# A chain of four attention layers on one core: high and low parts of small heads in every third row, and the maxima's rows sent by GpSimd

## The reference

```
L1: x = x + cross_attention(layernorm(x), ctx), 16 heads of 16; x = x + mlp(layernorm(x))
L2: x = attention(queries x, keys and values of concat(ctx, x)), 16 heads of 16, 512 keys, + residual; rmsnorm; mlp
L3: grouped attention, 32 query heads of 8 channels on 8 key heads, with an added mask; + residual; layernorm
attention: softmax(q k^T * scale + mask) v, all in float32
```

## Time and profile before

| | us |
|---|---|
| median of 3 runs | 1466.15 (1464.59 to 1468.97) |
| the profiled execution | 1463.16 |
| its span | 1461.9 |
| PE busy | 1295.2 (89%) |
| DVE busy | 902.7 (62%) |
| ACT busy | 722.1 (49%) |
| POOL busy | 456.4 (31%) |
| mean granted clock of TensorE | 0.916 |

### The profile page before, as it was taken

One profiled execution on the slowest core, in us unless ns is written; L12 is line 12 of the kernel. 1 busy time (PEld: TensorE's weight loads), 2 busy tenths in 40 slices (PEclk: granted clock), 3 DMA queues, 4 the chain that ended last, 5 costly groups with the idle time before them and its releaser, 6 DMA issues. The chain is left out here.

```text
span 1461.9 us, 26853 instructions
## 1 busy us (share of the span) xinstructions
PE 1295.2 (89%) x9901; PEld 1100.8 (75%) x9901; DVE 902.7 (62%) x2341; ACT 722.1 (49%) x1817; POOL 456.4 (31%) x843
## 2 busy tenths in 40 slices
PE   6999999999999999998777779776878898879795
PEld 6999999999999999987745458544545686556463
DVE  6966666698756666886755656545545455446461
ACT  5766656678656666672133442234534422434342
POOL 3544445454534544443321131210100211002101
PEclk9999999999999999999967799779877896989998
DMA  5310000033000000031333113155130222121200
GB/s 167 106 55 2 1 1 5 1 101 110 23 2 1 2 1 2 32 114 32 47 48 46 24 45 52 19 71 67 25 47 2 76 33 42 30 34 35 31 2 16
DMA packets 40356, 56.65 MB, mean 39 GB/s; under 512 B 5536, under 2 KB 20832, under 8 KB 40224
## 3 DMA queue, kind: packets, MB, share of 16 engines
q1 hardware_dynamic: 40224, 54.92, 18.6%
HBM read 32.68 MB, written 1.05 MB: 23 GB/s over the span
## 5 line engine op out<-in xcount | busy, mean ns | idle before, releaser
L1807 ACT ACTIVATE PT<-bank 128x512 f32<-128x512 f32 x320 | 174.6, 595 | 193.9 <-PE bank L1749 107.5
L1078 POOL TENSOR_SCALAR E<-E,rl 128x256 f32<-128x256 f32 x256 | 237.9, 941 | 0.0
L1871 DVE CUSTOM_DVE_ANT_0 Em<-bank,M 128x256 bf16<-128x256 f32 x256 | 95.1, 420 | 101.2 <-issue 65.8
L821 ACT ACTIVATE QTh<-bank,bqs 128x256 fp32r<-128x256 f32 x128 | 60.7, 474 | 182.1 <-PE bank L117 182.1
L1864 DVE TENSOR_REDUCE nm<-bank 128x1 f32<-128x512 f32 x128 | 82.3, 684 | 94.1 <-PE bank L1718 93.9
L1076 POOL TENSOR_TENSOR pb<-E,rl 128x2 f32<-128x2 f32 x128 | 33.7, 263 | 326.6 <-DVE rl L954 326.6
L1903 POOL CAST np<-nm 128x8 fp32r<-128x8 f32 (+1 forms) x80 | 15.1, 188 | 342.2 <-DVE nm L1864 141.9
L1741 PE MATMUL bank<-Q,K 51*128 51x256 f32 (+1 forms) x640 | 98.1, 325 | 26.2 <-DMA Q<-rows 20.4
L831 ACT ACTIVATE E<-bank,nm 128x257 f32<-128x257 f32 x256 | 119.3, 480 | 3.1 <-DVE nm L931 3.1
L938 DVE SCALAR_TENSOR_TENSOR QTl<-bank,bqs,QTh 128x256 fp32r<-128x256 f32 x128 | 61.8, 483 | 84.6 <-ACT KT L822 83.9
L1764 PE MATMUL bank<-PT,V 128*32 128x256 f32 x1280 | 107.2, 475 | 2.6 <-ACT PT L1807 2.6
(11 more groups left out here) (464 smaller groups left out, 4485.6 us busy)
## 6 DMA issues: line engine op xcount, KB each, us to landing
stage<-in_wts SPq DMA_DIRECT2D x99, 256.0 KB, 3.1
Q<-stage SPq DMA_DIRECT2D x72, 128.0 KB
K<-stage SPq DMA_DIRECT2D x48, 128.0 KB
K<-xh SPq DMA_DIRECT2D x16, 128.0 KB, 8.7
Q<-rows SPq DMA_DIRECT2D x96, 4.0 KB
K<-stage SPq DMA_DIRECT2D x24, 64.0 KB
X<-in_x SPq DMA_DIRECT2D x4, 256.0 KB, 5.8
stage<-in_ctx SPq DMA_DIRECT2D x4, 256.0 KB, 3.6
```

Source lines behind the costliest of these rows:

```text
L1078: m = pool.tensor_scalar(s.E[:, i % 3, t, 0:256], s.E[:, i % 3, t, 0:256], s.rl[:, r, t:t + 1], None, ALU.mult)
L1807: act.activation(s.PT[i % s.NPT][:, 2 * u:2 * u + 2, :].rearrange("p a b -> p (a b)"), s.STB[y][:], ACT.Exp).then_inc(S["t_ex"])
L1871: dve.tensor_tensor_reduce(out=s.Em[:, (2 * i + e) % 4], in0=s.SB[y][:, e * 256:e * 256 + 256], in1=s.M3[:, j, e, :], scale=-1.0, scalar=3 ...
```

## The change

`spread` writes the part number n (0, 1, 2) to partitions 64y+n, 64y+n+3, and so on up to 64y+n+3(d-1), instead of the block from 64y+nd. Q and K are laid out alike, so the same products are summed, in another order. Mask and maxima rows stay where they were. `maxima_rows` leaves `heads_sp` and stands in `heads_pool`, where step p sends the rows of step p-1's turn before the maxima of the step are split. Which data it waits for, the sizes and the destinations are as before. In `take_rest` one condition is written twice, which changes nothing.

```
@@ spread, in heads_prep_sp
         for y in range(2):
-            at = 64 * y + n * d
+            at = slice(64 * y + n, 64 * y + n + 3 * d - 2, 3)
             src = P[64 * y:64 * y + 64] if rows == 128 else P[0:64, 0, :]
-            sp.dma_start(f32(dst[at:at + d]), f32(src)).then_inc(S[sem], 16)
+            sp.dma_start(f32(dst[at]), f32(src)).then_inc(S[sem], 16)
@@ heads_sp
-    def maxima_rows(g):
...
     for p in range(s.steps()):
-        for g in s.turns_at(p):
-            maxima_rows(g)
         b, steps = s.preps(p)
@@ heads_pool
+    def maxima_rows(g):
+
+        b, pair, n = g * s.G // s.nh, g * s.G % s.nh // 2, s.G // 2
+        w.wait_ge(S["t_rows"], s.o["g"] + g + 1)
+        for y in range(2):
+            at = 64 * y + s.R
+            pool.dma_start(f32(s.Q[b % s.NR][at:at + 2, pair:pair + n, :]),
+                           f32(s.rows[4 * n * y:4 * n * y + 4 * n, g % 2, :])).then_inc(S[f"dma_rows{g % 2}"], 16)
+
...
     for p in range(s.steps()):
+        for g in s.turns_at(p - 1):
+            maxima_rows(g)
         for g in s.turns_at(p):
             maxima_parts(g)
```

More of the change, by code:

```diff
@@ L1206, in take_rest @@
             self.Em = sb("Em", [128, 4, 256], BF16)
+        if self.l == 3:
             self.identR = sb("identR", [128, 128], F32R)
```

## The result

| | before | changed |
|---|---|---|
| median, us | 1467.37 (4 runs, 1464.59 to 1468.97) | **1412.93** (4 runs, 1412.02 to 1414.72) |
| ratio | | **0.963**, 95% interval 0.961 to 0.965 |
| span of the profiled execution | 1461.9 | 1410.7 |
| mean granted clock | 0.916 | 0.930 |

What follows compares the result with a forecast made beforehand. PE was taken as the bound, with 45.9 us of waits for transfers. Stage 3 27.0, stage 2 18.8, stage 1 2.9 and POOL 0 made 48.7 us, said as 48: 1466.15 becomes 1418 us, range 1402 to 1447.

Steps and rivals of the forecast that it cites:

- The bound: PE, busiest everywhere, loses 45.9 us waiting for transfers: 20.4 in stage 3, 19.8 in stage 2, 5.7 in stage 1.
- Measuring from turn to turn: Stalls sized between PE's turns to include the slow clock afterwards: 27.0 us in stage 3, 18.8 in stage 2.
- Part 1: Spreads into every third row: 160 GB/s per unit of share instead of 119; stage 2's land some 6 us earlier.
- Part 2: Maxima's rows issued by POOL: SP loses 160 issues and 80 waits, spreads start a step or two earlier.
- rival A: Spreads' rate stays as it is; earlier starts and SP's freed queue still give 43 us, 1423; chance 0.14.
- Stage 1: Both waits for Q's spreads end; half of 5.7 us counted, 2.9 us.
- POOL: POOL's added 160 issues, at 1.0 us each, are hidden under PE's step and cost 0 us.
- the slack: Room for POOL's two issues between PE's turns: up to 1.6 us an issue in stage 2, 1.9 in stage 3.
- rival C: POOL becomes the bound: slower from 2.3 us an issue, 1484 us at 2.5; chance 0.10.
- Rival B: Rows queue behind spreads on the transfer engines, whoever issues: stage 2 18.8 us, stage 3 about 7; 1440; chance 0.07.

Runs made afterwards that it cites:

- part 1 alone: Against the kernel before: Q and K parts in every third row, maxima's rows still issued by SP; 1412.8 us, ratio 0.963.
- part 2 alone: Against the kernel before: maxima's rows issued by POOL, Q and K parts still in blocks; 1439.9 us, ratio 0.981.
- seven memsets: Changed kernel with seven small memsets on POOL in front of the two issues of each group; 1519.4 us, ratio 1.036 to the kernel before.
- four memsets: Changed kernel with four small memsets on POOL in front of the two issues of each group; 1445.4 us, ratio 0.986 to the kernel before.

## Why the prediction was right, and where it was not

**The bound** was read rightly: 45.9 us of waits of PE for transfers, and the time went where they went. The gain by stage is within 1.4 us of the forecast in stages 2 and 3. But "these are the batch changes and nothing else" holds for stages 1 and 2 alone. In stage 3 PE waited in the middle of a batch, at the fifth of its eight turns (1243.96 to 1255.97 in the earlier trace rows is the first), for rows of its own batch that were late while the next batch's twelve spreads flew.

**Measuring from turn to turn** was right. The waits of stage 3 are 20.4 us, the gain is 25.6: the steps after a stall run at a lower clock, and that time is won back with the wait. Over the 8 to 10 us behind its three stalls the kernel before was granted 0.77, 0.72 and 0.81. By the changed kernel's own turns the three were worth 6.8, 10.2 and 9.6 us (forecast 6.8, 10.1, 10.1). In stage 2 the first was held against the wrong turn, 4.68 where the same turn now takes 3.47, and was worth 6.9 us instead of 5.7.

**Part 1: the rate** was mis-sized. I took 160 GB/s, midway between 119 and SP's limit; the spreads have 313 and 295 per unit of share, which is my upper bound, the rate of loads (307). The time came out even so, with some luck: 187 in every second row gave the same time, but 160 itself was not run. The map of ports was no better guide to stage 2 and a good one to stage 3. The Trainium skill (SBUF — State Buffer, "Door 1: The DMA port swizzle") puts four neighbouring partitions on a port, and partitions 32 apart on the same one. By that map each transfer has:

| destination of a transfer | ports, most rows on one | GB/s per share |
|---|---|---|
| block of 16 (stage 2) | 4, 4 | 119 |
| block of 8 (stage 3) | 2, 4 | 139 |
| 16 every third row | 8, 3 | 313 |
| 8 every third row | 6, 2 | 295 |
| 8 every fourth row | 8, 1 | 300 |
| 8 every eighth row | 4, 2 | 245 |

The last column is from the windows above and the earlier trace rows, one window for each. The trace agrees with the map in this: the two slow rows of the table are those with four rows on a port, and every eighth row, whose two rows on a port are 32 apart, is below every fourth, with one, as I had expected of it (200 to 280). The number of ports doesn't order them (139 on 2, 119 on 4), and neither does the most on one (245 and 295 both with two). The size comes out in stage 3 alone: twice the rate was promised and 2.1 times measured, while for stage 2 a third more was promised and the runs show 2.6 times. What makes the step from three to four so large is open.

**Part 2** is where the mechanism was off, though the sum did not suffer. That "the spreads start a step or two earlier" came true and more: 7.6 us in stage 3 and 6.7 in stage 2, against part 1 alone. But the prediction has two reasons for the late transfers and a part of the change for each, and once part 1 is there, part 2 is worth nothing that these runs can tell (both ratios are 0.963, known to some 3 and 5 us). Alone part 2 is worth 28 us, and rival A had counted 43 for it. It gave stage 3 its 27 us, because "the rows no longer wait for twelve issues"; the runs show 11. Rows sent at once still fly up to 11.8 us behind spreads into blocks, and with every third row in stage 3 and the rows on SP that stage gains 26 us. So there the flight made the rows late and not the queue. In stage 2 was read rightly: the 8.5 us for which row transfers hold SP count as long as the spreads are slow, and taking them away leaves 0.9 of 19.8 us of waits. The two parts are two cures for one stall, 55 and 28 us alone and 54 together.

**Stage 1** was halved for want of a row, 2.9 against 7.1; this is most of what the forecast of 48 lacks. Two waits are left, of up to 1.9 us, where there were two of up to 3.7. The windows over the stage, before and changed:

```profile
725.83:841.02 115.19, 83.22 (x587) 55.41 (x587) 65.90 (x129) 44.83 (x99) 22.91 (x50) 0.73 0.30 43
```

```profile
726.64:834.69 108.05, 79.94 (x588) 54.11 (x588) 66.02 (x129) 44.84 (x99) 39.77 (x80) 0.76 0.14 46
```

PE waits 2.0 us less for transfers and is busy 3.3 us less at a higher clock; the latter I had counted in stages 2 and 3 and left out here. A wait of 1.9 us on nothing that the profile names is gone too. The other kernels with third rows, but for the one with seven memsets, took 108.3 to 111.0 us in this stage, so up to 3 us of the 7 may be chance.

**POOL** at 0 us was right: two issues take 1.1 us, 0.56 each, below the lower bound I had from SP (0.61). But the slack was stated too widely. I took 4.68 us as the closest turns of stage 2 from one pair in the earlier trace rows; the closest are 3.70, and the same formula then gives (3.70 - 1.0 - 0.5) / 2 = 1.1 us an issue, not 1.6. With four memsets an issue costs (1.1 + 2.3) / 2 = 1.7 us, and the formula of rival C asks 3 us of it; the run shows 28 in stages 2 and 3. The round itself was sized well (1.0 + 0.5 + 2 x 1.7 = 4.9 us against the 5.05 seen); what was missing were the short turns. Stretching each turn of stage 2 below 5.05 us to that length adds 11.8 us, an estimate from the turns of the changed kernel, of the 17 lost. PE's waits for the splitting grew by 16 us and the time by 32, with a mean clock of 0.919 for 0.930. Between 1.7 us (21 us faster than before) and 2.55 (52 us slower) a straight line crosses zero at 1.9 us, an estimate; I had put rival C's break-even at 2.3.

**Rival A** (the rate stays) is out by the windows. **Rival B** (the rows queue behind the spreads, whoever issues them) is half true, and its 1440 us is what part 2 alone took. It gave 18.8 us to stage 2 and 7 to stage 3, where 16 and 11 were measured. POOL's rows flew up to 11.8 us behind spreads into blocks, and at most 4.7 in the changed kernel; ScalarE's flew 7.7 and 7.8 behind blocks. So part 1 cleared the way for the rows. The Trainium skill (DMA: Bandwidth & Descriptors, "Back-pressure in remote DMA") says of transfers between cores that a saturated port at the destination backs up to the source's engine and stalls its other queues too. On one core these flights look like that; whether data or completions are held was not tested. The rule of the Trainium skill that I had made into this rival (the same page, "Issuing engines are not separate DMA queues"), that issuers share the engines and a second one saves issue time alone, agrees with these runs: the flights were as long from ScalarE as from POOL, and once the engines were free, moving the issues saved nothing (1412.8 against 1412.9 us).

## What to carry to other kernels

When two edits attack the same stall, price each one alone and again with the other in place: the second may be worth nothing. Here a window with a share near 1 and few GB/s was the sign of a slow layout of the destination, and spreading the partitions beat reordering the queue; once they were spread, the issuing engine was the limit. Before counting slack on an engine, list the distances of all the steps that it must keep up with, not one pair.

## What the runs showed of the hardware

- The same bytes between the same buffers moved at 119 GB/s per unit of share into blocks of 16 partitions, and at 313 into every third. With two parts in every second row and one in a block it was 187. For 8 partitions it was 139 in blocks, 295 in every third, 300 in every fourth and 245 in every eighth.
- POOL issues a small transfer inside SBUF in 0.56 us (544 to 804 ns) and it lands 1.7 us later in the median; SP's issue of a spread took 0.61 us in the median.
- One wait of 1.85 us was followed by at least 8 us at a granted clock of 0.50, and the two turns around it stood 5.9 us further apart than in the changed kernel (13.0 against 7.0). Around two waits of like length, 1.76 and 1.89 us, it was 2.9 and 3.7 us.
- Transfers of 4 KB from POOL's queue flew up to 11.8 us while spreads into blocks were under way, and from ScalarE's 7.8; the median of all of POOL's, of 2 and 4 KB, was 1.7 us.
